# A fused attention and gated feed-forward layer on one core: turned tiles, query pieces and the gate's low parts in other places

## The reference

```
xn = layernorm(x)
q, k, v = xn @ Wq.T, xn @ Wk.T, xn @ Wv.T       # 16 query heads, 4 key/value heads, 64 wide
att = softmax(mask(q @ k.T / 8))                 # causal, window of 512, first 4 keys always open
s = (att @ v) @ Wo.T
# feed-forward part on the last row of each batch
thought = in_norm(xn)[:, -1, :] @ agg_w + agg_b
4 times: thought += gelu(norm(thought) @ d1_w + d1_b) @ d2_w + d2_b
out = xn + sigmoid(xn @ gate_w + gate_b) * (thought @ bc_w + bc_b)
g = silu(layernorm(out))
result = x + s * g
```

## Time and profile before

| | |
|---|---|
| median of 3 runs | 2237.75 us |
| lowest and highest | 2233.9 and 2241.33 us |
| the profiled execution | 2241.33 us, its span 2239.6 us |
| granted TensorE clock, mean | 0.991 |
| busy: PE, DVE, ACT, POOL | 96%, 66%, 38%, 11% of the span |
| PE matmuls | 13433 |
| DMA | 366.57 MB, 164 GB/s |

### The profile page before, as it was taken

The page is one execution under the profiler, slowest core; times in us unless marked ns, Lnnn a source line. Parts: engine busy times, 40 slices in busy tenths (PEclk is TensorE's granted clock), DMA queues, the critical chain, the costliest instruction groups (busy, mean ns, idle before and its releaser), DMA issues. The chain is left out here.

```text
span 2239.6 us, 35984 instructions
## 1 busy us (share of the span) xinstructions
PE 2158.8 (96%) x13433; PEld 1605.7 (72%) x13433; DVE 1467.3 (66%) x3265; ACT 840.9 (38%) x1793; POOL 239.3 (11%) x510
## 2 busy tenths in 40 slices
PE   7999999999999999999999999988999999999998
PEld 6666666766666676666676666657888888888886
DVE  6465677665667657567665566585676676767767
ACT  2254554444554435455343445462111111111111
POOL 2100111010002011011101000010101010010100
PEclk9999999999999999999999999999999999999999
DMA  7486459533447734545853354545333334243331
GB/s 255 137 275 216 129 186 298 167 134 120 152 159 251 245 104 149 179 137 193 283 173 119 122 185 165 201 165 184 141 109 144 122 122 143 101 150 99 144 132 56
DMA packets 174383, 366.57 MB, mean 164 GB/s; under 512 B 13320, under 2 KB 111880, under 8 KB 159904
## 3 DMA queue, kind: packets, MB, share of 16 engines
q1 hardware_dynamic: 168240, 348.30, 46.6%
q0 software_dynamic: 5568, 14.79, 1.9%
q10 hardware_dynamic: 432, 1.57, 0.2%
HBM read 284.79 MB, written 79.72 MB: 163 GB/s over the span
## 5 line engine op out<-in xcount | busy, mean ns | idle before, releaser
L805 ACT ACTIVATE pt<-t_ps 128x512 f32<-128x512 f32 x432 | 237.4, 595 | 475.4 <-PE t_ps L1090 474.9
L1022 PE MATMUL j_ps<-x_hi,w 128*128 128x512 f32 x1232 | 411.4, 404 | 0.0
L814 ACT ACTIVATE probs<-probs,neg_max 128x660 f32<-128x660 f32 (+5 forms) x512 | 356.8, 703 | 45.3 <-DVE neg_max L1344 45.0
L1344 DVE CUSTOM_DVE_ANT_0 probs<-s_ps,mask 128x660 f32<-128x660 f32 (+5 forms) x512 | 322.2, 667 | 68.4 <-PE s_ps L1057 66.6
L1747 PE MATMUL out_ps<-wo,w 128*128 128x512 f32 x1536 | 353.4, 389 | 2.6 <-DVE w L1804 2.6
L1747 PEld LDWEIGHTS out_ps<-wo,w 128*128 128x128 f32 x1536 | 288.3, 188 | 62.7 <-issue 3.0
L1747 PE MATMUL gate_ps<-x_hi,w 128*128 128x512 f32 x1024 | 281.5, 391 | 4.8 <-PEq L468 4.8
L1022 PEld LDWEIGHTS j_ps<-x_hi,w 128*128 128x128 f32 x1232 | 231.0, 190 | 54.4 <-issue 6.6
L1090 PE MATMUL t_ps<-ident,probs 128*128 128x128 f32 x1728 | 240.6, 280 | 24.4 <-DVE x_lo L1332 12.2
L1057 PE MATMUL s_ps<-k_hi,q 64*128 64x330 f32 (+5 forms) x1664 | 251.5, 330 | 8.8 <-DVE q L1316 5.6
L1057 PEld LDWEIGHTS s_ps<-k_hi,q 64*128 64x128 f32 x1664 | 160.0, 185 | 118.8 <-issue 61.6
(11 more groups left out here) (182 smaller groups left out, 2317.5 us busy)
## 6 DMA issues: line engine op xcount, KB each, us to landing
fw<-in_L_ffn_d_w_dram SPq DMA_DIRECT2D x128, 1024.0 KB, 5.3
w<-WT SPq DMA_DIRECT2D x36, 1024.0 KB, 5.7
w<-XS SPq DMA_DIRECT2D x64, 512.0 KB, 6.4
XS<-x_hi SPq DMA_DIRECT2D x32, 512.0 KB, 6.9
XS<-x_lo SPq DMA_DIRECT2D x32, 512.0 KB, 8.0
Y<-y SPq DMA_DIRECT2D x256, 64.0 KB, 2.1
b_x<-in_L_attn_x_dram SPq DMA_DIRECT2D x32, 512.0 KB, 4.1
b_y<-Y SPq DMA_DIRECT2D x32, 512.0 KB, 6.5
```

The costliest lines, as they stand in the source:

```text
L805: act.activation(pt[:, m % PT_SLOTS, :, :], bank[:, :].rearrange("p (h q) -> p h q", q=P), ACT.Copy).then_inc(pt_ready, 1)
L814: act.activation(probs[:, slot, 0:width], probs[:, slot, 0:width], ACT.Exp, bias=neg_max[:, slot:slot + 1], scale=-1.0, accum_out=row_sum[ ...
L1022: last = pe.matmul(bank_of((kind, b, n)), w[:, slot, wp * C + c * P:wp * C + c * P + P], xs[:, c, bass.ts(ch, BANK)], start=i == 0, stop=i ...
L1344: dve.tensor_tensor_reduce(out=probs[:, slot, 0:width].rearrange("p (a n) -> p a n", a=parts), in0=s_ps[head % 2][:, :].rearrange("p (a n) ...
```

## The change

- The turned tile of a step goes on PE from in front of the second scores to in front of the values (behind place 2), and its parts on ACT and DVE from the middle of the step to behind place 2. It uses the banks in another turn (`x_bank`), and the first two turned blocks of the same step's probabilities now wait for `x_taken`.
- Query pieces 14 and 15 of each batch, which were made in steps 24 and 25, are made in two parts each in steps 22 to 25.
- Query piece 1 of batches 1 to 3 is made at place 3 of the step in front of the batch, and no longer at place 0 of its first step.
- The gate's low parts go from DVE to POOL, in front of the step's `pack_sinks`.

```diff
-                   20: (12, 0, STEPS), 21: (13, 0, STEPS), 24: (14, 0, STEPS), 25: (15, 0, STEPS)}
+                   20: (12, 0, STEPS), 21: (13, 0, STEPS),
+                   22: (14, 0, 14), 23: (14, 14, STEPS), 24: (15, 0, 14), 25: (15, 14, STEPS)}
...
-            if s == 0 and b:
-                found[0] = ("q", b, 1, 0, STEPS)
...
                     found[0], found[2] = ("k", b + 1, 1, 0, STEPS), ("q", b + 1, 0, 0, STEPS)
+                    found[3] = ("q", b + 1, 1, 0, STEPS)
...
-            return t_ps[(turns_before(u - 1) + min(turns_of((u - 1) % TB), 2) + half) % 2][:, :]
+            return t_ps[(turns_before(u) + half) % 2][:, :]
...
+                        if b == B - 1:
+                            for k in GATE_AT.get(s, ()):
+                                pool.wait_ge(gate_high, k + 1)
+                                pool.wait_ge(j_full, NUMBER["q", B - 1, 4 * KV - 1] + 1)
+                                pool.wait_ge(xs_stored, 32 * TB * B)
+                                pool.tensor_tensor(x_lo[:, k, :], xn[k % 2], x_hi[:, k, :].bitcast(F32),
+                                                   ALU.subtract).then_inc(gate_split, 1)
                         if has_sink(unit_of(s)[1]):
                             pack_sinks(UNITS * b + s)
...
-                        wait_taken(*turn_two_ago(u - 1, min(turns_of((u - 1) % TB), 2) + half))
+                        wait_taken(*turn_two_ago(u, half))
...
-                    for step_no in (u, u + 1):
-                        item = turned_in(*divmod(step_no, UNITS))
-                        if item and (step_no == u or i >= 2):
-                            pe.wait_ge(x_taken, 2 * turned_no(item) + 2)
+                    item = turned_in(*divmod(u, UNITS))
+                    if item and i < 2:
+                        pe.wait_ge(x_taken, 2 * turned_no(item) + i + 1)
...
-                    if turned_in(b, s):
-                        turn_later(u, turned_in(b, s))
                     scores(b, s, 1)
                     turn_two(2)
                     fill(1)
                     turn_two(4)
                     fill(2)
+                    if turned_in(b, s):
+                        turn_later(u, turned_in(b, s))
                     if u:
                         values(u - 1)
                     fill(3)
...
-                    if b == B - 1:
-                        for k in GATE_AT.get(s, ()):
-                            dve.wait_ge(gate_high, k + 1)
-                            dve.tensor_tensor(x_lo[:, k, :], xn[k % 2], x_hi[:, k, :].bitcast(F32),
-                                              ALU.subtract).then_inc(gate_split, 1)
```

More of the change, by code:

```diff
@@ L832, in step @@
                     take_place(0)
-                    if turned_in(b, s):
-                        for half in range(2):
-                            turned_high(u, turned_in(b, s), half)
                     for i in range(2, min(n, 4)):
@@ L843, in step @@
                     take_place(2)
+                    if turned_in(b, s):
+                        for half in range(2):
+                            turned_high(u, turned_in(b, s), half)
                     take_place(3)
@@ L1473, in step @@
                         add_sums(b, s)
-                    if turned_in(b, s):
-                        for half in range(2):
-                            turned_low(u, turned_in(b, s), half)
                     mask_scores(b, s, 2)
@@ L1490, in step @@
                     take_place(2)
+                    if turned_in(b, s):
+                        for half in range(2):
+                            turned_low(u, turned_in(b, s), half)
                     take_place(3)
```

## The result

The changed kernel took 2227.22 us (median of 22 runs) against 2241.01 us for the kernel before in the same sessions. The ratio is 0.9947, with a 95% interval of 0.9937 to 0.9957: 11.9 us faster, a little over half of the 22.2 us forecast. The profiled execution took 2227.23 us (span 2225.5). One of the 22 runs took 2674 us at a lower granted clock, as single runs of some later kernels did; the ratios leave such runs out.

The account below looks back on a forecast made before the run. TensorE is busy 2158.8 of 2239.6 us, so only its waits can go: 31.1 - 13.4 + 2.5 + 2.0 (overlap) = 22.2 us faster, from a median of 2237.75 to 2215.5 us, range 2204 to 2230.

Parts of the forecast that it names:

- Removed waits, 31.1 us: PE's waits for turned low parts, sinks, L1084, probs and query pieces end: 16.9 + 4.6 + 2.0 + 3.4 + 4.2 us, 46 waits.
- New waits, 13.4 us: Steps 22 to 29 and batch starts: 0.2 + 1.2 + 0.25 + 1.6 + 0.85 + 0.35 = 4.45 us, times three batches.
- Step 25 is the worst: VectorE frees the tile's first half at 6.1 us, PE comes at 4.7: wait 1.4 us, 1.6 with the second half.
- the things that would make the prediction wrong: Turned low parts above 15 us, VectorE waiting for the x tile's load, or a gate gain above 4.5 us.
- Part 3: Query piece 1 into the step before its batch: 4.2 us of waits go; a 0.35 us wait comes at each fold.
- Part 4: Gate's low parts on POOL: 4.0 us of waits for `y` go, 1.5 come at the sinks' packs, net 2.5.
- rival B: POOL takes operands ahead of the divides, three races at 2.5 us and as much on packs: 2223 us, chance 0.2.
- parts 1 and 2: Turned tiles behind query pieces end 16.9 us of waits; pieces 14 and 15 over steps 22 to 25 end 4.6, 2.0 and 3.4.
- The forecast case: The likeliest case: 22.2 us faster, median 2215.5 us, chance 0.45.
- C: Rival: waits only change places as VectorE hands its lateness from step to step; gain about 6 us, 2232 us, chance 0.08.
- D: Rival: nearly no new waits, 6 and not 13.4 us, and packs in time; 2206 us, chance 0.2.
- rival A: Turned tiles' low parts late in all steps 22 to 29, slower than before; 2248 us at 1.6 us a tile, chance 0.07.

Follow-up runs that it names:

- the two kernels with 8 and 16 products: Changed kernel, piece 15 as 8 and 16 products, weights' load later, split first, last gate part on VectorE: 2216.46 us; with all gate parts on VectorE: 2218.15 us.
- the load's experiment: Changed kernel with SP's load of the value weights' first half moved one step later, to step 25: 2217.69 us, ratio 0.9907 to the kernel before.

## Where the prediction was right and where it failed

- **Removed waits, 31.1 us: right.** All 46 are gone. Batch 0, steps 1 to 21, is 5.8 us shorter, where 4.7 and some overlap were forecast.
- **New waits, 13.4 us: near as VectorE's own chain, wrong as a whole.** In the kernel with the weights' load later the five entries (turned low part 5.7, sinks 3.2, ACT's copy 1.9, fold and split) are 13.4 us. That this is the forecast sum to the tenth is luck. It is made up otherwise: the first turns of steps 26 and 27 1.25 and 0.63 where I had 1.6 for step 26 alone, ACT's copy 0.63 for 0.85, step 23 1.07 for 1.2, nothing for the 0.2 of step 22 and the 0.25 of step 24, and POOL's split, 0.5, which I didn't have. In the change they are 19.5 us and bring stretches at half clock.
- **The step that failed** is the term "Step 25 is the worst ... 1.4 us, and 0.2 for the second half: 1.6 us", worked out with VectorE's operations alone. The first turn alone waited 2.94, 2.95 and 3.94 us, and 1.0 to 2.0 us were lost in slow products behind each. The x tile's load was named among the things that would make the prediction wrong, with the remark that it is issued about 1 us later, and was priced at nothing. I had looked at who issues it and not at what SP issues ahead of it. SP waits for query piece 14 and then loads the value weights; part 2 lets that wait end a step earlier. Moving this load alone brings 9 us by the ratios, where 10.3 were missing, and the 1.25 us that are left at the first turn are near the 1.4 that the term had for it.
- **Part 3, 3.15 us net: wrong.** The waits for `q` went and the fold's 0.33 us came as forecast, but POOL's split stood behind the thought's small power. With the split first, steps 31 and 0 give 0.83 of the 1.05 us per batch.
- **Part 4, 2.5 us net: nothing came, neither in the change nor alone.** The price on POOL was near: 2.45 us in the mean against the 2.56 taken.

```profile
L756 POOL TENSOR_TENSOR x_lo<-xn,x_hi 128x1024 fp32r<-128x1024 f32 x8 | 19.5, 2450 | 45.7 <-ACT x_hi L857 45.7
```

  The 4.0 us for `y` went, too. What I missed is late next: the feed-forward weights' load (waits of 0.9 and 1.35 us: PE wanted it 6.6 us after its issue, and in the kernel before, held up by the wait for `y`, used it 9.2 us after), and rival B's race came true once, 2 us, on a pair of merges; the divides that B named keep their 0.89 us. The Trainium skill, "SBUF — State Buffer", the section "SBUF: two separate sides", describes the port pair that VectorE and GpSimd share as a lock held for a whole instruction: VectorE's pair ends 0.16 us behind POOL's operation, so the trace agrees. The Trainium skill, "GPSIMD Engine Reference", section 3.1, has 4497 ns for an addition of 2048 elements; half of it is an estimate of 2.25 us, and the subtraction here took 2.45.
- **The terms don't close.** The load (9 us), part 3 (about 3) and part 4 (2.5) are together more than the 10.3 us that were missing. With the load later, steps 22 to 30 of batches 0 and 1 are 4.7 us shorter than before, where the forecast's terms make about 3.3 a batch (7.0 us of waits go, 4.1 come, 0.4 of overlap), so parts 1 and 2 gave some 4 us more in three batches than they were costed at. Which term was too small there stays open.
- **The chances.** The forecast case described a 2215.5 us kernel. What came lies between it and C, by a mechanism that none of the cases had, so that it lies inside the range is luck. D's few new waits didn't come, and rival A, slower than before, wasn't near.

## What to carry to other kernels

When work moves to an earlier step, follow every semaphore that its end releases: here a load on another engine's queue waited for it, went out 6.7 us earlier in its step, and was ahead of a tile that was needed sooner. When waits are taken out of a stretch, the loads in it lose that much cover. Ask of each how long it has from issue to use, before and after (11.7 us, then 5.7). And a move that is worthless alone (0 us for the turned tiles) can be part of the whole gain with another (15 us with the query pieces), so cost such a pair together, and measure each of them alone.

## What the chip showed that I had not expected

- A wait can cost more than its length. Behind PE's 2.95 us of nothing the granted clock fell to 1.2 GHz and 12 products took 4.03 us in place of 2.99; in the three batches step 26 lost 3.3, 3.2 and 5.2 us for 1.7, 1.7 and 2.7 us of wait. But it doesn't happen behind every wait of such a length. In step 27 of batch 0 of the two kernels with 8 and 16 products PE waited 2.51 and 2.49 us, and behind the wait the trace has (the columns are those of the load's experiment, the clock the last but two)

```profile
371.60:375.00 3.40, 3.39 (x14) 3.08 (x15) 2.04 (x6) 2.15 (x5) 0.00 (x0) 0.53 1.02 417
364.50:368.00 3.50, 3.48 (x22) 3.03 (x23) 2.05 (x6) 2.62 (x6) 0.00 (x0) 1.00 1.03 413
```

  so the first step took 16.5 us and the second 15.1.
- An x tile of 512 KB took 7.3 us to land behind two loads of 1024 KB, and 4.4 us when one of the two came later. The two loads are SP's and the tile is POOL's: that they are issued by different engines didn't keep them apart.
- VectorE's light merge of 0.48 us for a pair took 2.62 us next to one POOL operation with two operands, the mirror image of the cast in the earlier trace rows.
